# A decoder layer's expert stage: from dense experts over all tokens to picks sorted by expert through DRAM

## What is computed

```python
scores = (jnp.einsum('btd,ed->bte', x, router_w) + router_b) / temp
gates = _sinkhorn(scores)                      # 3 rounds over experts and over tokens
topk_vals, topk_idx = jax.lax.top_k(gates, K)  # K = 2 of E = 8
topk_gates = topk_vals / (jnp.sum(topk_vals, axis=-1, keepdims=True) + 1e-08)
g = jax.nn.relu(jnp.einsum('btd,edf->btef', x, wg))
p = jnp.einsum('btd,edf->btef', x, wp)
all_out = jnp.einsum('btef,efd->bted', g * p, wo)     # FF = 256, D = 128
gathered = jnp.take_along_axis(all_out, topk_idx[..., None], axis=2)
expert_out = jnp.sum(gathered * topk_gates[..., None], axis=2)
return x + expert_out
```

## Time and profile before

| | us |
|---|---|
| median of 3 runs (lowest to highest) | 421.45 (420.58 to 422.46) |
| the profiled execution, its own time | 422.17 |
| span of that execution, first to last instruction | 420.4 |
| PE busy, share of the span | 356.0, 85% |
| DVE busy | 262.3, 62% |
| ACT busy | 146.0, 35% |
| POOL busy | 144.6, 34% |
| DMA, mean rate | 57 GB/s |

### The profile page before, as it was taken

How to read it: one execution, slowest core, us unless ns; L and a number is a source line. 1 busy time by engine, 2 the same in 40 slices (tenths; PEclk the granted TensorE clock), 3 DMA queues, 4 the chain that set the end, 5 groups by cost and what they waited for, 6 DMA issues and landing times.

```text
span 420.4 us, 5562 instructions
## 1 busy us (share of the span) xinstructions
PE 356.0 (85%) x1896; PEld 235.4 (56%) x1909; DVE 262.3 (62%) x628; ACT 146.0 (35%) x276; POOL 144.6 (34%) x150
## 2 busy tenths in 40 slices
PE   1546678579987999779996899999999899999995
PEld 1333345343464535445454543687788688888883
DVE  6595376882297924971249831576779766666662
ACT  2503404816634265005531146222221323223221
POOL 7331213562012130011003020356354565666563
PEclk9985676979999999999798799999899999999998
DMA  4203650331004210153001200321100242220000
GB/s 109 68 1 81 174 192 1 94 72 38 2 0 115 54 37 0 40 122 93 0 2 50 94 16 2 125 51 50 50 27 25 68 123 69 82 64 26 27 0 25
DMA packets 22216, 23.84 MB, mean 57 GB/s; under 512 B 5117, under 2 KB 17341, under 8 KB 21973
## 3 DMA queue, kind: packets, MB, share of 16 engines
q1 hardware_dynamic: 21805, 23.29, 20.2%
q10 hardware_dynamic: 384, 0.20, 0.2%
HBM read 20.11 MB, written 3.18 MB: 55 GB/s over the span
## 4 chain that ended last, share of the span: by engine, by line
PE 60%; DVE 21%; ACT 5%; issue 4%; DMA 4%; POOL 4%; ACTq 1%; SPq 0%; POOLq 0%; DVEq 0%
DVE nmax_mask L984 6%; PE pC L1337 4%; PE pS L1322 4%; PE pC L1334 4%; PE pS L1319 3%; PE pS L268 3%; PE pS L270 3%; PE pS L269 3%; PE pG L1116 2%; PE pS L1286 2%; PE pA L268 2%; PE pS L1289 2%; PE pB L268 2%; PE pB L270 2%; PE pB L269 2%
## 5 line engine op out<-in xcount | busy, mean ns | idle before, releaser
L586 POOL TENSOR_TENSOR xi_lo<-xi_f,xi_hi 128x512 fp32r<-128x512 f32 x43 | 55.8, 1299 | 53.4 <-ACT xi_hi L739 53.2
L984 DVE TENSOR_REDUCE nmax_mask<-pS 128x3 f32<-128x462 f32 (+1 forms) x96 | 52.7, 578 | 18.1 <-PE pS L1289 17.2
L707 ACT ACTIVATE prob<-pS 128x512 f32<-128x512 f32 x80 | 42.4, 600 | 33.4 <-PE pS L1322 30.3
L739 ACT CAST xi_hi<-xi_f 128x512 fp32r<-128x512 f32 x43 | 26.7, 621 | 65.8 <-DVE xi_f L1039 65.8
L1039 DVE TENSOR_TENSOR xi_f<-sig,pS 128x512 f32<-128x512 f32 x64 | 44.0, 688 | 3.9 <-PE pS L270 0.6
L1286 PE MATMUL pS<-k_stack,q_stack 72*128 72x154 bf16 x256 | 36.7, 249 | 3.2 <-DMA q_stack<-q_scr 3.1
L586 POOL TENSOR_TENSOR act_lo<-xi_f,act_hi 128x512 fp32r<-128x512 f32 x21 | 27.5, 1310 | 27.1 <-ACT act_hi L739 27.1
L1289 PE MATMUL pS<-mbias,ident_bf 128*128 128x462 bf16 (+1 forms) x96 | 36.3, 378 | 0.0
L1286 PEld LDWEIGHTS pS<-k_stack,q_stack 72*128 72x128 bf16 x256 | 22.0, 107 | 12.1 <-issue 7.1
L1283 PE MATMUL pS<-mbiasT,ident_bf 128*128 128x128 bf16 x72 | 17.5, 243 | 11.7 <-DVE nmax_mask L984 11.4
L739 ACT CAST act_hi<-xi_f 128x512 fp32r<-128x512 f32 x21 | 13.0, 620 | 41.0 <-DVE xi_f L1039 41.0
(11 more groups left out here) (332 smaller groups left out, 846.3 us busy)
## 6 DMA issues: line engine op xcount, KB each, us to landing
prob<-w_scr SPq DMA_DIRECT2D x16, 256.0 KB, 3.3
q_stack<-q_scr SPq DMA_DIRECT2D x9, 384.0 KB
q_scr<-q_parts SPq DMA_DIRECT2D x12, 128.0 KB, 2.4
k_stack<-k_scr SPq DMA_DIRECT2D x36, 40.0 KB
res<-in_x_dram SPq DMA_DIRECT2D x4, 256.0 KB, 4.6
prob<-in_L_ffn_wg_dram SPq DMA_DIRECT2D x1, 1024.0 KB, 5.9
prob<-in_L_ffn_wp_dram SPq DMA_DIRECT2D x1, 1024.0 KB, 8.3
ctx_in<-in_L_ffn_wo_dram SPq DMA_DIRECT2D x4, 256.0 KB, 3.1
```

Source lines behind the costliest of these rows:

```text
L586: pool.tensor_tensor(hid_lo[u % NHID], hid[:, u % 2, :], f32(hid_hi[u % NHID]), ALU.subtract).then_inc(s_hidlo, 1)
L707: act.activation(prob[:, (NSB * b + n) % NBUF, :], score_bank(b, NSA + n)[:, :], ACT.Exp).then_inc(s_exp, 1)
L739: act.copy(hid_hi[u % NHID], hid[:, u % 2, :]).then_inc(s_hidhi, 1)
L984: dve.tensor_reduce(nmax[:, qt, hs[0]:hs[-1] + 1], score_bank(b, n)[:, 0:len(hs) * KEYS].rearrange("p (h k) -> p h k", k=KEYS), AX.X, ALU. ...
```

## The change

- Picks instead of all experts. The router's result is no longer a gate for every expert but, for each token, two picks. The 2 × 512 picks of a batch are sorted by expert. Three groups are sorted by themselves: batches 0 and 1, batch 2, batch 3 (`GRP`). Within a group each expert's picks fill whole tiles of 128 rows. The number of tiles is fixed at the worst case: 23 + 15 + 15 = 53. Rows that no pick fills are blank and their outputs are dropped.
- Placing. `rank` (a scan on DVE, three small products on PE) counts earlier picks of each expert, `place` (20 small DVE operations a group) makes the row of each pick, the expert of each tile and the two gates.
- Through DRAM. SP first fills `sort_scr` with blank rows, 14 transfers of 3.5 MB together (`fill_rows`). POOL scatters the normalized rows with a row number appended, 516 B a row, by indirect DMA: 128 rows in each, 16 + 8 + 8 transfers (`scatter`). SP loads them back in 14 chunks of up to four tiles (`sorted_rows`, three buffers).
- A tile. PE transposes the 128 rows (`sort_T`), ACT and DVE split them. `up` has the rows as stationary operand and the expert's gate and up weights, 512 columns together, as the moving one: three passes. ACT rectifies (256 columns), DVE multiplies (256 columns) without the gate. PE transposes the hidden tile twice (`hid_T`), ACT copies it, and `down` makes two plain float32 products of 128 columns. ACT copies out, and POOL scatters 128 output rows to `out_scr` (53 transfers). `hid_T`, `down` and the copies go in pairs of tiles. The split of the hidden features and of the output weights is gone, and so are the gate rows.
- The expert of a tile is a number in a register: PE loads it from SBUF (`value_load`) before each `up`, and the weights' addresses are worked out from it.
- Back. When all tiles that hold a batch's picks are scattered and have landed, SP loads the two picked outputs of each token (`combine_in`), DVE adds them with their gates in eight operations of 128 × 128 (`combine`), and SP stores.
- Order. The layer norm, the split and now the logits of batch 2 move to earlier slots of the last attention batch (`POST_LAST_AT`); `rank` and `place` of group 0 and 18 router steps of group 1 are added to that batch; `place` of group 1, the end of batch 3 and the router of group 2 lie between tiles 0 and 27. `combine` of batches 0, 1 and 2 stand in DVE's order at tiles 31, 32 and 47.

```diff
+    GRP = [(0, 2), (2, 1), (3, 1)]
+    NG = len(GRP)
+    GROUP_OF = [g for g, (_, nb) in enumerate(GRP) for _ in range(nb)]
+    GB = max(nb for _, nb in GRP)
+    PICKS = 2
+    NTILES = [(PICKS * nb * S + E * (P - 1)) // P for _, nb in GRP]
+    TILE0 = [sum(NTILES[:g]) for g in range(NG + 1)]
+    NT = TILE0[NG]
+    CH = 4
+    CHUNKS = [(g, t0, min(CH, TILE0[g + 1] - t0)) for g in range(NG) for t0 in range(TILE0[g], TILE0[g + 1], CH)]
...
+        wgp = [sb("wgp_hi", [P, E, 2, FF], F32R), sb("wgp_lo", [P, E, 2, FF], F32R)]
...
+        ROUTER2_AT = [10, 11, 11, 12, 12, 13, 13, 14, 14, 15, 16, 16, 17, 18, 18, 19, 20, 20, 21, 21, 22, 23, 24, 24, 25,
+                      27, 25]
+        COMBINE_AT = [(9, "in", 0), (9, "in", 1), (10, "out", 0), (10, "out", 1),
+                      (NC, "in", 2), (NC, "out", 2), (NC, "in", 3), (NC, "out", 3)]
+        ADD_AT = [(31, 0), (32, 1), (47, 2)]
+        AHEAD = 3
...
+        for j in range(2 * NPAIR + 4):
+            if j >= 2 and j + AHEAD in first_up and first_up[j + AHEAD] > 1:
+                STEPS.append(("sort_T", first_up[j + AHEAD], 0))
+            if j < NT:
+                STEPS.append(("up", j, 0))
+                STEPS += left[j]
+            if j % 2 == 1:
+                k = j // 2 - 1
+                if 0 <= k - 1 < NPAIR:
+                    STEPS.append(("down", k - 1, 0))
+                if 0 <= k < NPAIR:
+                    STEPS.append(("hid_T", k, 0))
+        STEPS.append(("combine", NB - 1, 0))
...
+                elif step == "fill_rows":
+                    sp.wait_ge(s_blank, 2)
+                    _, t0, nt = CHUNKS[n]
+                    sp.dma_start(sort_scr[t0 * P:(t0 + nt) * P, :].rearrange("(n p) c -> p n c", p=P),
+                                 blank[:, :].unsqueeze(1).broadcast_to([P, nt, ROW])).then_inc(s_filled, 16)
...
+            def combine_in(b):
+                end = (TILE0[GROUP_OF[b] + 1] - 1) // 2
+                for buf in range(NY):
+                    sp.wait_ge(s_back[buf], landed(buf, end))
+                if b >= 2:
+                    sp.wait_ge(s_add, PICKS * T * (b - 1))
+                for k in range(PICKS):
+                    rows = out_scr[(k * NB + b) * S:(k * NB + b + 1) * S, :]
+                    sp.dma_start(picked[b % 2][:, k, :, :], rows.rearrange("(t p) d -> p t d", p=P)
+                                 ).then_inc(s_picked[b % 2], 16)
...
+            for c, (g, t0, n) in enumerate(CHUNKS):
+                first, nb = GRP[g]
+                sp.wait_ge(s_in[g], 16 * PICKS * T * nb)
+                if c >= NSLOT:
+                    sp.wait_ge(s_sortT, c - NSLOT + 1)
+                    sp.wait_ge(s_meta, c - NSLOT + 1)
+                sp.dma_start(sorted_rows[c % NSLOT][:, 0:n, :],
+                             sort_scr[t0 * P:(t0 + n) * P, :].rearrange("(t p) c -> p t c", p=P)
+                             ).then_inc(s_sorted[c % NSLOT], 16)
+                combining(c)
+            combining(NC)
...
+                elif step == "scatter":
+                    first, nb = GRP[b]
+                    if b == 0:
+                        pool.wait_ge(s_filled, 16 * NC)
+                    pool.wait_ge(s_pos, PLACE_STEPS * b + PLACED)
+                    pool.wait_ge(s_extb, (PICKS + 1) * (first + nb))
+                    for i in range(nb):
+                        for t in range(T):
+                            for k in range(PICKS):
+                                blk = t * nb + i
+                                pool.indirect_dma_start(
+                                    out=sort_scr[:, :],
+                                    out_offset=bass.IndirectOffsetOnAxis(ap=pick_row[k][b][:, blk:blk + 1], axis=0),
+                                    in_=ext_of(first + i, k)[:, t, :], in_offset=None,
+                                    bounds_check=NT * P - 1, oob_is_err=False).then_inc(s_in[b], 16)
+                elif step == "sort_T":
+                    _, t0, nt = CHUNKS[b]
+                    pool.wait_ge(s_sorted[b % NSLOT], 16 * (b // NSLOT + 1))
+                    pool.tensor_copy(meta[:, t0:t0 + nt], sorted_rows[b % NSLOT][:, 0:nt, D]).then_inc(s_meta, 1)
+                elif step == "down":
+                    pool.wait_ge(s_y, b + 1)
+                    pool.wait_ge(s_meta, CHUNK_OF[pair(b)[-1]] + 1)
+                    for i, j in enumerate(pair(b)):
+                        pool.indirect_dma_start(
+                            out=out_scr[:, :],
+                            out_offset=bass.IndirectOffsetOnAxis(ap=meta[:, j:j + 1].bitcast(I32), axis=0),
+                            in_=expert_y[b % NY][:, i, :], in_offset=None,
+                            bounds_check=PICKS * NB * S - 1, oob_is_err=False).then_inc(s_back[b % NY], 16)
...
+                elif step == "up":
+                    act.wait_ge(s_up, b + 1)
+                    if b >= 2:
+                        act.wait_ge(s_hid, b - 1)
+                    act.activation(relu[:, b % 2, :], pUp[b % 2][:, 0:FF], ACT.Relu).then_inc(s_relu, 1)
...
+            def combine(b):
+                g = GROUP_OF[b]
+                nb = GRP[g][1]
+                dve.wait_ge(s_picked[b % 2], 16 * PICKS * (b // 2 + 1))
+                dve.wait_ge(s_res, b + 1)
+                for k in range(PICKS):
+                    dve.wait_ge(s_add, PICKS * T * b + T * k)
+                    for t in range(T):
+                        blk = t * nb + b - GRP[g][0]
+                        dve.scalar_tensor_tensor(out=res[:, b, t, :], in0=picked[b % 2][:, k, t, :],
+                                                 scalar=pick_w[k][g][:, blk:blk + 1], in1=res[:, b, t, :],
+                                                 op0=ALU.mult, op1=ALU.add).then_inc(s_add, 1)
...
-            def up(b, n):
-                u = N * b + n
-                e, hf = divmod(n, HF)
-                cols = slice(hf * P, (hf + 1) * P)
-                x3_b = [half[:, b, :] for half in x3]
-                if u >= 2:
-                    pe.wait_ge(s_gated, u - 1)
-                three_pass(pe, pGate[u % 2][:, :], wgp[0][:, 0, e, cols], wgp[1][:, 0, e, cols], x3_b[0], x3_b[1]
-                           ).then_inc(s_gp, 1)
-                if u >= 2:
-                    pe.wait_ge(s_hid, u - 1)
-                three_pass(pe, pUp[u % 2][:, :], wgp[0][:, 1, e, cols], wgp[1][:, 1, e, cols], x3_b[0], x3_b[1]
-                           ).then_inc(s_up, 1)
-            def down(b, n):
-                u = N * b + n
-                w_hi, w_lo = (half[:, n * D:(n + 1) * D] for half in woP)
-                ps = pO[b % 2][:, :]
-                pe.wait_ge(s_hidhi, u + 1)
-                if n == 0 and b >= 2:
-                    pe.wait_ge(s_add, b - 1)
-                elif n == 0 and b == 1:
-                    pe.wait_ge(s_x2, NB)
-                    pe.wait_ge(s_logit, GROUPS)
-                pe.matmul(ps, w_hi, hid_hi[u % NHID], start=(n == 0), stop=False, skip_group_check=True)
-                pe.matmul(ps, w_lo, hid_hi[u % NHID], start=False, stop=False, skip_group_check=True)
-                pe.wait_ge(s_hidlo, u + 1)
-                pe.matmul(ps, w_hi, hid_lo[u % NHID], start=False, stop=(n == N - 1), skip_group_check=True
-                          ).then_inc(s_down, 1)
+            def up(j, e):
+                c = CHUNK_OF[j]
+                col = (j - CHUNKS[c][1]) * P
+                x_hi, x_lo = (half[:, c % 2, col:col + P] for half in sortT)
+                w_hi, w_lo = (half[:, :, :, :].rearrange("p e w f -> p (e w f)")[:, bass.ds(e * (2 * FF), 2 * FF)]
+                              for half in wgp)
+                three_pass(pe, pUp[j % 2][:, :], x_hi, x_lo, w_hi, w_lo).then_inc(s_up, 1)
+            def down(j, e):
+                for h in range(HF):
+                    col = (j % 2) * FF + h * P
+                    last = pe.matmul(pO[:, (j % 2) * D:(j % 2 + 1) * D], hidT[:, (j // 2) % 2, col:col + P],
+                                     wo_sb[:, bass.ds(e * (HF * D) + h * D, D)], start=(j % 2 == 0 and h == 0),
+                                     stop=(h == HF - 1), skip_group_check=True)
+                last.then_inc(s_down, 1)
...
+                    pe.wait_ge(s_pos, PLACE_STEPS * CHUNKS[CHUNK_OF[b]][0] + NAMED)
+                    experts[b] = pe.value_load(tile_expert[0:1, b:b + 1], min_val=0, max_val=E - 1)
+                    pe.wait_ge(s_sortlo, CHUNK_OF[b] + 1)
+                    if b >= 2:
+                        pe.wait_ge(s_hid, b - 1)
+                    up(b, experts[b])
```

636 lines of the change are left out of this document (377 added, 259 removed).

## The result

| | median of the runs | runs |
|---|---|---|
| before | 421.01 us | 417.47 to 422.46 |
| after | 439.57 us | 438.88 to 441.72 |

The ratio is 1.046, with a 95% interval of 1.039 to 1.054. The change is slower by 18.6 us where 26 us less were forecast, outside the range of 371 to 430. The profiled execution took 439.48 us with a span of 437.5, against 420.4 before.

What follows compares the result with a forecast made beforehand. PE was taken to set the expert stage's pace. First tile at 278.0 us, tiles at 1.45 us, one DVE wait of 7.6 and an end of 14.4 gave a span of 393.4, forecast 395 us, range 371 to 430.

Steps and rivals of the forecast that it cites:

- PE's work, removed and added: Expert stage: 132.5 us of PE's work removed, 53 tiles at 1.45 us (76.9 us) added; PE alone would give 55.6 us.
- Start of the stage: Ahead of the experts: stage starts 11.4 us later, at 276.3 us, and the first tile stands at 278.0 us.
- the 10.4 us for DVE's work: Last attention batch, between its maxima: 5.6 us moved from batch 2's end plus 4.8 for group 0's rank and place.
- the 1 for the fill: Ahead of the stage: the row maxima's transfer may meet the blank rows' burst, between 0 and 2.2 us, 1 taken.
- the 1.7 of startup: Before the first tile: four transposes, ACT's copy 0.59 and DVE's split 0.69, together 1.7 us.
- POOL's scatters: Time one indirect transfer holds POOL: bounds 0.48 to 2.4 us, 1.04 taken, so a tile's scatter hides behind PE's 1.45.
- Rival C: POOL becomes the bound: span 304.6 + 69 c, c being one scatter's time; slower, about 430 to 470 us; chance 0.10.
- Tiles 0 to 31 and the new wait: Tile 31's up ends at 339.1 us; DVE then waits 7.6 us for combine of batch 0, behind POOL's scatters.
- The end: Behind the last up: its down, copies, last scatter, landing, load, combine and store, together 14.4 us.
- Register load: PE's load of each tile's expert before up: bounds 0 to 2.2 us, taken as nothing, hidden behind the product ahead.
- Rival E: The clock falls: a third of the tiles at half clock costs 26 us, giving 421 us; chance 0.04.
- "Slower": Whole kernel slower than before, by POOL as the bound, exposed register loads or a falling clock; chance 0.18.

Runs made afterwards that it cites:

- a_sp: The changed kernel with the 32 transfers of the picks issued by SP as plain ones in token order, without the sort; 412.1 us, 0.981 of before.
- a_tick: The changed kernel with group 0's scatters spread singly, groups 1's and 2's between tiles, and a one-element-a-row copy behind all 85 scatters; 428.4 us, 1.022 of before.
- a_ny8: The changed kernel with 8 buffers for pairs of output tiles in place of 4, nothing else; 443.1 us, 1.057 of before.
- a_plain: The kernel of a_sp with the 53 output scatters as plain POOL transfers too, so no indirect transfer is left; 406.6 us, 0.969 of before.
- a_sp_const: The kernel of a_sp with each tile's expert a program constant (tile number modulo 8) in place of a register load; 414.2 us, 0.988 of before.

## Why the prediction was wrong

- **PE's work, removed and added.** Right. The dense passes are gone and a tile costs about what the sum said: 1.54 us beside its share of waits against 1.45.
- **Start of the stage.** Forecast for the first tile 278.0, measured 296.27. Of the 18.3 us, 12.2 are the scatters of group 0 (296.27 against 284.08 in a_sp; with the scatters spread and a copy behind each, a_tick has 283.80), which the step put at nothing without a row for it: it put them on POOL, where they hide, and took the engines around them as untouched. **This is the step that failed.** What the runs showed in its place is the copy of the row maxima, 4.8 us behind PE's transposes while the scatters run, and PE at half clock around it. The other 6.1 us are there without them (284.08 in a_sp): the 10.4 us for DVE's work, the 1 for the fill and the 1.7 of startup were too low together. The startup alone was 3.2 (from 280.85 to 284.08 in a_sp); I did not take the rest apart.
- **POOL's scatters.** The bounds held, the size was off: 1.28 us, not 1.04. Rival C's own formula, 304.6 + 69 c, gives 392.9 at that c, so POOL alone did not pace. Its signs were half there: POOL's queue without a gap, and ACT's output copies late. But it was not buffers that were missing, as a_ny8 shows.
- **Tiles 0 to 31 and the new wait.** The wait for combine(0) that the prediction worked out at 7.6 us is not to be seen in after, where DVE comes there only at 382.55; with the late signals cured it appears at 7.2 us (a_tick). The mechanism was right; that 7.2 comes so near 7.6 is luck, since c was larger and a_tick's scatters stand between the tiles. The waits for the rows of groups 1 and 2, 7.6 and 6.1 us in a_tick, were missing: the step counted POOL's queue against combine(0), not against the loads of the next group. Nor did it see that SP's queue holds the load of batch 3's rows behind the loads for combine, 5.5 us in a_sp.
- **From the first tile to the end.** Forecast 115.4 us (278.0 to 393.4), measured 141.2. Of the 25.8 us, 6.2 are there without any indirect transfer (285.25 to 406.8 in a_plain is 121.6), 4.5 come with the outputs' scatters (126.0 in a_sp) and 15.2 with the picks'. a_tick, which cures the late signals and puts the scatters between the tiles, got none of the 15.2 back (141.5).
- **The end.** 14.4 us behind PE's last `up`, measured 19.7 (417.84 to 437.5). The last scatter ends at 427.57, 9.7 us behind the product, where the step's terms up to it sum to 3.3. The step let one `down` follow the last `up`, but the order of steps leaves five tiles' `down` behind it and two more outputs uncopied: the last output is copied by 424.48, 6.6 us behind, for which the terms give 2.3. Then its scatter stands 2.1 us behind the six others on POOL. Landing, load, combine and store took 9.9 in place of 11.1. The receipt is as the prediction had it: SP's load went out 2.25 us after the start of the last scatter, and POOL did not sit through it (1.28). An estimate by the fit in the Trainium skill (DMA: Bandwidth & Descriptors, Anatomy of one DMA, SWDGE path), 2.0 us plus 64 KB over 436 GB/s, is 2.15, close to it.
- **Register load.** Right: covered (a_sp_const). That a floor of 0.6 us, as the Trainium skill states it (DMA: Bandwidth & Descriptors, Latency and other measured facts), would stay hidden agrees with that run.
- **Rival E**, the clock: half clock follows the stalls of PE, as in 240 to 265 at 0.57. It was a consequence here: without the late signals the same stretch has 0.72 in a_tick and 0.73 in a_sp. From 285 to 320, where most tiles run without a stall, the changed kernel has 0.98, thin products and all.
- **The chances.** "Slower" had 0.18, all of it in a POOL that paces, in register loads and in the clock. A row of scatters that delays TensorE's signals to other engines was in no rival, and nothing in the trace of before could show it, since it has no indirect transfer. The unknown was bounded as a price of one instruction (0.48 to 2.4 us); that a new kind of instruction might cost something outside its own queue had no chance at all.

By runs, the 44.6 us between forecast and result fall into three: 11.6 are in a_plain, which has no indirect transfer at all (406.6 against 395; 7.3 of it ahead of the first tile, and a wait of 5.65 for batch 3's rows behind), 5.5 are the scatters of the outputs, and 27.4 those of the picks. Of these 27.4, the 12.2 ahead of the first tile are shown to be a row of scatters beside engines that depend on TensorE; the 15.2 behind it are shown only as a sum.

## What to carry to other kernels

An instruction that no trace of the kernel holds needs two prices, its own time and what it does to the others; measure the second by putting a row of it, awaited by nobody, into the kernel as it is. Don't let GpSimd issue a long row of indirect transfers while other engines depend on TensorE: five cost nothing here, twelve 6.3 us, and a 0.2 us copy behind each one was enough. Here that, with the first row spread, gave back 11.2 of the 18.6 us and no more: rows that go through DRAM in groups want their scatters early enough for the next group's first load, not only for the combine, and a load queue that doesn't hold them behind another wait.
